# First cross-attention of a two-layer decoder: one pass tile by tile, integers transposed by DMA

## The reference

```python
q = (x @ Wq + bq).reshape(1, B * N, H, hd)
kv = (cond @ Wkv + bkv).reshape(1, -1, 2, H, hd)
k, v = (kv[:, :, 0], kv[:, :, 1])
...
q = _fq_sym(q, axis=-1)
k = _fq_sym(k, axis=-1)
v = _fq_sym(v, axis=2)
attn = jnp.einsum('bhqd,bhkd->bhqk', q, k)
attn = jax.nn.softmax(attn.astype(jnp.float32), axis=-1)
attn = _fq_unsigned(attn, axis=-1)
out = jnp.einsum('bhqk,bhkd->bhqd', attn, v)
return out @ Wp + bp
```

## Time and profile before

| | |
|---|---|
| median of three runs | 3246.03 us |
| lowest and highest run | 3238.53 and 3249.94 us |
| the profiled execution | 3243.19 us |
| its span | 3241.3 us |
| PE, DVE, ACT busy over the span | 86%, 63%, 53% |
| the three stages of the first cross-attention | 896.35 to 1876.40 us of the span |

### The profile page before, as it was taken

The page is one execution under the profiler, slowest core; times in us unless marked ns, Lnnn a source line. Parts: engine busy times, 40 slices in busy tenths (PEclk is TensorE's granted clock), DMA queues, the critical chain, the costliest instruction groups (busy, mean ns, idle before and its releaser), DMA issues. The chain is left out here.

```text
span 3241.3 us, 61186 instructions
## 1 busy us (share of the span) xinstructions
PE 2794.4 (86%) x20357; PEld 1828.0 (56%) x20564; DVE 2030.5 (63%) x4457; ACT 1721.1 (53%) x2944; POOL 304.9 (9%) x356
## 2 busy tenths in 40 slices
PE   4999999999965888888888689789978879999997
PEld 2777777777743555555555445455545545555654
DVE  4677777777678999999999621366646642323232
ACT  1555555555555999999999311266635531111110
POOL 1121212212100000000000000011112310000000
PEclk9999999999997999999999689899989989999999
DMA  4000000000020000000000100100002200000000
GB/s 168 1 1 0 0 0 0 0 0 0 0 83 5 0 0 0 0 0 0 0 0 0 42 13 0 22 0 0 0 25 70 60 2 1 0 0 0 0 0 26
DMA packets 35593, 42.36 MB, mean 13 GB/s; under 512 B 3220, under 2 KB 32720, under 8 KB 34512
## 3 DMA queue, kind: packets, MB, share of 16 engines
q1 hardware_dynamic: 30968, 33.86, 3.4%
q10 hardware_dynamic: 4568, 7.74, 0.6%
HBM read 35.29 MB, written 2.10 MB: 12 GB/s over the span
## 5 line engine op out<-in xcount | busy, mean ns | idle before, releaser
L2360 DVE TENSOR_TENSOR f_h<-f_act_g,f_p_u 128x512 f32<-128x512 f32 (+1 forms) x132 | 90.7, 687 | 517.2 <-PE f_p_y L2253 451.4
L1355 PE MATMUL x_p_s<-x_kT,x_qz 128*128 128x512 bf16 x897 | 274.9, 387 | 127.1 <-DVE f_wg L1437 67.1
L2303 ACT ACTIVATE f_act_g<-f_p_g 128x512 f32<-128x512 f32 (+1 forms) x132 | 78.4, 597 | 548.0 <-PE f_p_g L2238 543.2
L1437 DVE TENSOR_SCALAR_CACHE_REDUCE f_wg<-x_p_s,x_nsq 128x1024 f32<-128x1024 f32 x256 | 318.6, 1282 | 51.7 <-issue 47.7
L1437 DVE TENSOR_SCALAR_CACHE_REDUCE f_wu<-x_p_s,x_nsq 128x1024 f32<-128x1024 f32 x256 | 327.4, 1279 | 12.9 <-PE x_p_s L1355 0.8
L1364 PEld LDWEIGHTS x_p_t<-identb,x_ints 128*128 128x128 bf16 x4096 | 242.0, 98 | 83.8 <-ACT x_turned L1423 43.9
L1414 ACT ACTIVATE x_ints<-f_wg,x_nb 128x2048 uint16<-128x2048 f32 x128 | 256.3, 2002 | 43.3 <-DVE x_nb L1454 43.3
L1364 PE MATMUL x_p_t<-identb,x_ints 128*128 128x128 bf16 x4096 | 274.2, 220 | 2.0 <-ACT x_turned L1423 2.0
L2238 PE MATMUL f_p_g<-f_xT,f_wg 128*128 128x512 f32 (+1 forms) x528 | 258.0, 612 | 16.8 <-ACT f_xT L2290 10.1
L1414 ACT ACTIVATE x_ints<-f_wu,x_nb 128x2048 uint16<-128x2048 f32 x128 | 256.3, 2002 | 0.6 <-DVE x_nb L1454 0.6
L1423 ACT COPY x_turned<-x_p_t 128x1024 int32<-128x1024 int32 x256 | 254.4, 994 | 2.5 <-PE x_p_t L1364 2.5
(11 more groups left out here) (354 smaller groups left out, 5229.5 us busy)
## 6 DMA issues: line engine op xcount, KB each, us to landing
x_qz<-x_zeros SPq DMA_DIRECT2D x16, 256.0 KB, 3.4
f_wg<-in_L_ffn_w_dram SPq DMA_DIRECT2D x2, 1408.0 KB, 7.4
f_wu<-in_L_ffn_w_dram SPq DMA_DIRECT2D x2, 1408.0 KB, 7.2
f_wd<-in_L_ffn_w_dram SPq DMA_DIRECT2D x1, 2816.0 KB, 10.6
a_wq<-in_L_attn_Wq_dram SPq DMA_DIRECT2D x1, 2048.0 KB, 10.7
a_wk<-in_L_attn_Wlk_dram SPq DMA_DIRECT2D x1, 2048.0 KB, 19.6
a_wv<-in_L_attn_Wlv_dram ACTq DMA_DIRECT2D x1, 2048.0 KB, 19.2
a_wo<-in_L_attn_Wo_dram ACTq DMA_DIRECT2D x1, 2048.0 KB, 24.6
```

The lines of the kernel that those rows point to most:

```text
L1355: mm = pe.matmul(p_s[half][:, c * BANK:(c + 1) * BANK], qz[:, par, :, :, :].rearrange("p a b t -> p (a b) t")[:, bass.ds(n, 1), :].rearran ...
L1437: dve.tensor_scalar(score[par][:, half, :], p_s[half][:, :], of_pass(nsq[:, par, :, :].rearrange("p a b -> p (a b)"), n), HIGHEST, ALU.mul ...
L2303: act.activation(act_g[n % 2][0:m, :], p_g[n % 2][0:m, :], ACT.Silu).then_inc(gate_up.sem, 1)
L2360: i = dve.tensor_tensor(h[n % 2][0:m, :], act_g[n % 2][0:m, :], p_u[n % 2][0:m, :], ALU.mult)
```

## The change

There are two stages in place of three. `x0_keys` goes over the context in eight rounds of two tiles and makes keys and values only. `x0_attend` does the rest for one query tile after another, with all 16 heads of a tile in a row. Its streams are written out whole, without loops: `jobs` places small pieces of the next tile's queries and of the last tile's output between the 16 units of a tile. The core of the diff, with the streams of SP, TensorE, ScalarE (the waits of `exps`), GpSimd and VectorE in this order:

```diff
-        qz = sb("qz", [P, 2, PAIRS, B, P], BF16)
+        svu, rsv = sb("svu", [P, H]), sb("rsv", [P, H])
...
-        x0_operands(core, qz, kT, vi, sv, nsq, att[:, :].rearrange("p (b h) -> p b h", b=B))
-        x0_attend(core, qz, kT, vi, nsq, att, esum, (ahead.wg, ahead.wu))
-        x0_output(core, sv, att, esum, ahead)
+        x0_keys(core, kT, svu, rsv, vraw)
+        x0_attend(core, kT, svu, rsv, vraw, ahead)
...
+    ROWS_KEPT, SLOTS, LATE = 4, 3, 6
+    PER_TILE = 2 * PAIRS
+    UNITS = B * PER_TILE
...
-        ints = [sb(f"ints{i}", [P, B, P], U16) for i in range(2)]
-        turned = [sb(f"turned{i}", [P, B, P], U16) for i in range(2)]
+        rows = [sb(f"row{i}", [P, 2, HALF]) for i in range(ROWS_KEPT)]
+        ints = [sb(f"ints{i}", [P, B * P], U16) for i in range(ROWS_KEPT)]
+        turned = [sb(f"turned{i}", [P, B, P], U16) for i in range(ROWS_KEPT)]
+        qz = [sb(f"qz{i}", [P, 2, PAIRS, P], BF16) for i in range(2)]
...
-        p_s = [ps(f"p_s{i}", [P, HALF]) for i in range(2)]
-        p_t = ps("p_t", [P, 2 * HALF], BF16)
-        p_o = ps("p_o", [P, BANK])
+        p_s = [ps(f"p_s{i}", [P, HALF]) for i in range(SLOTS)]
+        p_o, p_w = ps("p_o", [P, BANK]), ps("p_w", [P, BANK])
...
+            for u in range(UNITS):
+                k = u % ROWS_KEPT
+                sp.wait_ge(e_up, u + 1)
+                after(sp, o_made, u - ROWS_KEPT + 1)
+                sp.dma_start(turned[k][:, :, :], ints[k][:, :], transpose=True).then_inc(t_in[k], 16)
+                if u == PER_TILE:
+                    sp.wait_ge(v_up, 2)
+                    ahead.load(sp)
...
+            for u in range(UNITS + PER_TILE):
+                if u < UNITS:
+                    scores(u)
+                if 0 <= u - LATE < UNITS:
+                    values(u - LATE)
+                jobs(u, {1: [(turn_x, 1)], 3: [(project_q, 1)], 8: [(turn_reps, 1)], 11: [(turn_o, -1)], 13: [(project_o, -1)]})
...
+                act.wait_ge(nb_up, u + 1)
+                after(act, t_in[k], 16 * (u // ROWS_KEPT))
...
+                jobs(u, {4: [(integers, 1)], 5: [(scale_values, -1), (whole, 1)], 6: [(copies, 1)], 13: [(root, -1)], 14: [(norm, -1)]})
...
+                if u < UNITS:
+                    pass_over(u, 0)
+                jobs(u, {4: [(scale, 1), (denominators, -1)], 13: [(statistics, -1)], 14: [(variance, -1)]})
+                if u < UNITS:
+                    pass_over(u, 1)
+                    shift(u)
+                jobs(u, {3: [(largest, 1)], 4: [(inverse, 1), (divided, -1)], 12: [(residual, -1)], 13: [(moments, -1)]})
+                if u == ROWS_KEPT - 1:
+                    quantize_values()
```

More of the change, by code:

```diff
@@ new lines, in project @@
+            def project(i):
+                if not i:
+                    pe.wait_ge(loaded, 16)
+                pe.wait_ge(in_up.sem, in_up.of(i))
+                pe.wait_ge(k_read.sem, k_read.of(i - 1))
+                pe.wait_ge(v_read.sem, v_read.of(i - 1))
+                for j in range(2):
+                    at = p_kv[:, j * BANK:(j + 1) * BANK]
+                    pe.matmul(at, core.ones[:, :], core.bias("L0_xattn_bkv"), start=True, stop=False)
+                    for t in range(KT):
+                        mm = pe.matmul(at, inT[:, j * KT + t, :], wkv[:, t, :], start=False, stop=(t == KT - 1))
+                mm.then_inc(made.sem, 1)
@@ L1376, in emit @@
-            def emit(*passes):
-                line = [p and (*p, par) for p in passes for par in (1, 0)]
-                for par in range(2):
-                    here, _, earlier, oldest = (line + [None])[1 - par:][:4]
-                    if here:
-                        scores(*here, 0)
-                        scores(*here, 1)
-                    if earlier:
-                        turn(*earlier)
-                    if oldest:
-                        values(*oldest)
-            emit((0, 0), None, None)
@@ new lines, in scores @@
+            def scores(u):
+                b, j = divmod(u, PER_TILE)
+                a, par = divmod(j, 2)
+                if not j:
+                    pe.wait_ge(qz_up, b + 1)
+                for half in range(2):
+                    n = 2 * u + half
+                    after(pe, half_up, n - SLOTS + 1)
+                    for c in range(2):
+                        at = half * HALF + c * BANK
+                        mm = pe.matmul(p_s[n % SLOTS][:, c * BANK:(c + 1) * BANK], qz[b % 2][:, par, a, :], kT[:, a, at:at + BANK],
+                                       start=True, stop=True)
+                    mm.then_inc(s_made, 1)
@@ new lines, in values @@
+            def values(u):
+                b, h = divmod(u, PER_TILE)
+                k = u % ROWS_KEPT
+                if not u:
+                    pe.wait_ge(v_up, 2)
+                if not h:
+                    after(pe, o_read, b)
+                pe.wait_ge(t_in[k], 16 * (u // ROWS_KEPT + 1))
+                for c in range(B):
+                    mm = pe.matmul(p_o[:, h * XD:(h + 1) * XD], turned[k][:, c, :].bitcast(F16), vi[:, c, h * XD:(h + 1) * XD],
+                                   start=(c == 0), stop=(c == B - 1))
+                mm.then_inc(o_made, 1)
@@ new lines, in pass_over @@
+            def pass_over(u, half):
+                b, h = divmod(u, PER_TILE)
+                k = u % ROWS_KEPT
+                n = 2 * u + half
+                dve.wait_ge(s_made, n + 1)
+                if not half:
+                    after(dve, e_up, u - ROWS_KEPT + 1)
+                    if not h:
+                        dve.wait_ge(nsq_up, b + 1)
+                dve.tensor_scalar(rows[k][:, half, :], p_s[n % SLOTS][:, :], nsq[:, b % 2, h:h + 1], HIGHEST, ALU.mult, ALU.min,
+                                  accum_out=(low if half else hmin)[:, k:k + 1]).then_inc(half_up, 1)
```

625 lines of the change are left out of this document (292 added, 333 removed).

## The result

The changed kernel takes 3109.65 us (median of four runs, 3108.25 to 3115.07), the kernel before 3243.75 us on the same chip (3238.53 to 3249.94). The ratio is 0.9589, with a 95% interval of 0.9567 to 0.9610: 134 us less, where the prediction had 115. The profiled execution has a span of 3105.9 us against 3241.3.

A forecast was written before the change was run, and what follows sets the result against it. ScalarE was taken to bound the attention loop, VectorE next. Attention's terms sum to 786 us against 786.7 now; output stage (66) and keys (49) save 115 us, so 3243.2 becomes 3128 us, range 3085 to 3170 (0.60).

The forecast's parts named there:

- keys: First stage, keys only, two tiles a round: 127.25 us becomes 78 us, 49 saved.
- first tile's queries: Start of the attention, where nothing hides the first tile's queries: 15.5 us, 10 to 20.
- units: VectorE's passes in the attention: 256 units at 2.66 us, 681 us; 727 with 2.84.
- small pieces on VectorE: Ten small operations for each tile between VectorE's passes: 3.3 us a tile, 53 us for 16 tiles.
- values' long operations: Two long VectorE operations on the values, 4.42 and 2.29 us, move from the first stage into the attention: 6.7 us.
- waits at hand-overs: VectorE's pieces waiting for other engines in the attention: 0.5 us a tile, 8 us, range 0 to 30.
- feed-forward weights: 3 MB of loads in SP's queue ahead of transpositions, behind unit 16's: 7 us, 0 to 16.
- last tile's way out: End of the attention, last unit's exponential through output, projection and norm in sequence: 15 us, 12 to 20.
- the pace of bytes: Transposing DMA of 512 KB a unit, priced by plain transfers' rates: 1.7 to 2.7 us, hidden behind VectorE's passes.
- the far bound: Transposing DMA as 2048 packets of 256 bytes at 57 ns each: 7.3 us a unit, 4262 us in all.
- the rival was close: Transposing DMA sets the pace: over 2.87 us a unit, 3130 to 3240 us (0.08); over 3.3, slower (0.20).
- The argument against the rival: Rival: TensorE's clock falls in the attention and TensorE bounds at 3.1 us a unit, 60 us more, 3188 us; 0.07.

The follow-up runs named there:

- e2_half_turned: The changed kernel with only 8 of the 16 blocks of a unit transposed by DMA, each used twice by the values' matmuls: 3096.46 us, ratio 0.9545.
- e5_residual_later: The changed kernel with VectorE's residual add, and the statistics, root and norm after it, issued one unit later: 3094.03 us, ratio 0.9535.
- e1_turn_twice: The changed kernel with each unit's integers transposed by a second DMA too, into spare buffers that nothing reads: 3703.14 us, ratio 1.1415.
- e4b_before_order: The changed kernel with transposes back on TensorE, copied out by ScalarE, in the old loop's order of TensorE's work: 3197.07 us, ratio 0.9854.
- e11_copy_too: The changed kernel with a plain DMA copy of the same 512 KB to a spare buffer beside each transposition: 3502.85 us, ratio 1.0801.

## Why the prediction was right

| Term | predicted | measured |
|---|---|---|
| keys | 78 | 75.6 |
| first tile's queries | 15.5 | 13.6 |
| units | 681 | 679.7 |
| small pieces on VectorE | 53 | 28.7 |
| values' long operations | 6.7 | 6.7 |
| waits at hand-overs | 8 | 20.2 |
| feed-forward weights | 7 | 3.9 as a wait for scores, 6.8 by e2_half_turned |
| last tile's way out | 15 | 15.8 |

Without the second figure of the weights (which holds part of the waits at hand-overs) the right column has 844.2 us, and the windows 845.75. The predicted column has 864. The forecast of 3128 us was 18 us too high, and its range held: the mechanism came as forecast, the number partly by errors that cancel.

*The unit.* 2.66 us was taken from the two units ahead of the old loop, and not the 2.84 of the loop. It was 2.655. This one choice carries 46 us. The prediction gave the removed `p_o` copy, the written-out stream and ScalarE out of the way as reasons; how much each of them brings, no run separates.

*Small pieces.* This term was mis-sized: 3.3 us a tile as a sum of durations, 1.91 measured, and 16 tiles where the passes hold the pieces of 15 (the first tile's queries and the last tile's output are in the terms before and behind them). The timeline of the later four pieces of a tile, two of them shown:

```profile
1397.57 0.42 DVE L1546 TENSOR_TENSOR x_y<-x_p_w,x_res 128x256 f32<-128x256 f32 x1 [1.98 <-PE x_p_w L1382]
1397.91 1.28 DVE L1570 TENSOR_SCALAR_CACHE_REDUCE x_row<-x_p_s,x_nsq 128x1024 f32<-128x1024 f32 x1
...
1400.89 0.17 DVE L1555 BATCH_NORM_AGGREGATE x_mv<-x_stats 128x2 f32<-128x6 f32 x1
1400.99 1.28 DVE L1570 TENSOR_SCALAR_CACHE_REDUCE x_row<-x_p_s,x_nsq 128x1024 f32<-128x1024 f32 x1
```

An add of 0.42 us holds the next pass up by 0.34, an aggregation of 0.17 by 0.10: in these records an operation's last 0.07 or 0.08 us lie over the start of the next, and on a full engine a piece costs its start-to-start distance. The prediction added full durations and then 0.5 us of gaps, which do not exist here. Six pieces between 1414.34 and 1420.63 cost 0.98 us beyond two units of 2.655, and these four, from 1392.85 to 1403.72, cost 0.93 beyond three units and the wait of 1.98.

*Hand-overs.* Mis-sized in the other direction: 20.2 us for 8, inside its 0 to 30. The place was named (`residual` waits for the output's projection), and e5_residual_later shows that it is on the path. The two errors, 24 less and 12 more, partly cancel, which is luck.

*The DMA.* The result, nothing to pay, was right; the step that led to it was only half right. It took 1.7 to 2.7 us by the pace of bytes, since the packets of the earlier trace rows were already small. The measured 2.60 us lies at the upper end, and the packets are what the far bound supposed: 2,048 of 256 bytes. What was wrong in the far bound was the price of a packet: it took the 57 ns of a packet of 1.1 KB, where a packet of 256 bytes costs an engine 20.0 ns at the pace of e1_turn_twice. So the step that went by bytes came out right because smaller packets are cheaper, which it had no row for. A unit's time was 2.85 us, so the margin was 0.25 us: the rival was close, and that it did not come is partly luck. The issue was taken as 0.58 us; it is 2.24. Beyond the weights' tile, e2_half_turned shows no cost of it in the passes, with the issue at about half.

The Trainium skill (VectorE: DVE Perf Modes, section The three transpose paths) has 1309 ns a block by DMA; here 16 blocks in one DMA take 2.60 us, 163 ns a block. The way that the Trainium skill prefers where PSUM will do (the same page, section Rules for kernel authors), TensorE, was 87 us slower in e4b_before_order, where the copy out of PSUM falls on ScalarE, the bound. The 261 GB/s of the Trainium skill (DMA: Bandwidth & Descriptors, section Latency and other measured facts) is nearer: 512 KB in 2.60 us are 202 GB/s.

*The clock.* One mark of the prediction did not come: the clock is 0.75 over the passes, not 1.00, a mean between the levels of 1.2 and 2.4 GHz. The argument against the rival was wrong: it set waits under 1.3 us against the first stage, where the clock was 0.88. From 1250 to 1650 us TensorE is never idle for more than 1.35 us and the clock is 0.77, while in the kernel before idle stretches of 1.66 us recur through the first stage. Short waits alone did not keep the clock up. The rival's condition came half true and its price did not, since TensorE's 524 us of work leave it room in 741 and VectorE's passes waited 3.9 us for scores. The sum of the rival took the low level for all the time and TensorE's pieces as if nothing overlapped.

*Where the gain went.* The prediction had the attention's own window unchanged and the gain from the keys and the output stage. Its balance holds: queries, passes and tail take 770.1 us against 786.7 before, 16.6 less, and the other 117.7 us are the keys (51.6) and the output stage (66.1).

## What to carry to other kernels

When work is taken off the bounding engine, price the change by the next engine's step where nothing holds that engine up, and count a small piece by what it adds from start to start. Before a transfer is called hidden, get its pace, by issuing it twice, and set it against the time of the loop: the latency of one says little. Here the margin was 9%, and the next edits to VectorE's stream, with 11% less to do and to wait for, got 6% and ended on it.

## What the runs showed of the hardware

- A transposing DMA of 128x2048 two-byte elements inside SBUF goes at 2.60 us, in 2,048 packets of 256 bytes and 32 of 4 (e1_turn_twice), and a plain copy of the same bytes at 1.81 us beside it (e11_copy_too). The Trainium skill (Advanced Engine Details and Errata, section DMA Advanced Topics) has them equally fast; the runs decide: they are not.
- The issue of such a DMA lasts 2.24 us on SP in the median, 1.23 with half of the blocks (e2_half_turned), where a plain one of 512 KB takes 0.59 (e11_copy_too).
- TensorE's granted clock in the same stretch of the passes was 0.77 in the changed kernel, 0.85 with the values' matmuls doubled and 1.00 with the transposes back on TensorE. The first two take the same time to within 0.3 us.
